# A sandwich-norm layer of linear attention and a gated FFN: loads of two units moved ahead, and the order of the engines' work around the last blocks of a slot

## The chip, the cores and the metric

The kernel runs on one core of one Trainium2 chip. The metric is the device time of one execution in microseconds (us). The engines are TensorE (PE), VectorE (DVE), ScalarE (ACT), GpSimd (POOL) and SyncE (SP); SP here issues nearly all DMAs.

## The reference

`x` has the shape (4, 1024, 512), float32. What is computed, cut to what matters:

```
x = x + layernorm(attention(layernorm(x)))
x = x + layernorm(ffn(layernorm(x)))

attention: qkv = x @ w_qkv.T + b_qkv; 16 heads of 32; chunks of 128 tokens
  inter = (q * decay_q) @ S
  intra = ((q @ k.T) * dmask) @ v
  S = lam**128 * S + (k * decay_k).T @ v      (from chunk to chunk)
  out = (inter + intra) @ w_out.T + b_out
ffn: wq = w rounded to float8_e4m3 and back, for gate, up and down
  out = ((silu(x @ gate * gate_scale) * (x @ up * up_scale)) @ down) * down_scale
```

## The kernel before

The 4096 tokens are 16 units of 256 tokens (two tiles of 128, the index `t` or `c`); four units make a sequence. Float32 operands of matmuls are split into two float16 halves, `hi` (written by ScalarE) and `lo` (the rest, written by GpSimd or VectorE), so a product takes two or three matmuls. The order of work is written out by hand, for each engine by itself, and each engine runs its list in that order; semaphores (`x_lo_d`, `h_d`, ...) tie the lists together.

There are four stages.

- **ahead(k)**, k = 0 to 13 (`LEAD` = 14), one unit each: `x` is normalised (`moments_x`, `inverse_std_x`, `x_normalise`, `x_hi`, `x_lo`, two units before it is needed), turned by a DMA transpose (`turn_x`), projected to q, k (four banks, `project_qk(k, 0..3)`, line 692) and v (`project_v`, line 707), split, and written to DRAM (`spill_q`, `spill_k`, `spill_kd`, `spill_v`). Beside it the twelve pieces of the FFN's weights are loaded (`load_piece`) and rounded (`magic`, `rounded_sum`, `rounded`), their squares taken on ScalarE (`square(n)`, line 438, in unit n + 2) and summed by PE with a matrix of ones (`sum_squares`, line 671, between q/k and v of unit n + 2); the maxima of the sums (`norms`) set a scale of the FFN's values.
- **early(s)**, s = 0, 1: attention of unit s, projection of unit s + 14, and in early(1) the output projection (`project`, line 776) and first residual of unit 0.
- **slot(s)**, s = 2 to 15: attention of unit s, output projection of u = s - 1, and the FFN of v = s - 2. In slots 16 and 17 there is no attention, in 17 no projection either.
- In a slot PE runs `scores(0, 0)`, `carry_and_state(0)`, six blocks `gate_up(v, 0..5)` (line 799; a gate half and an up half of 16 matmuls each) with the remaining attention and `project` between them, and `down(v, 0)`, `down(v, 1)` (line 813).

The state of the attention goes from chunk to chunk: `carry_and_state(s, c)` on PE gives q times state and the new part of the state, VectorE adds it (`carry_and_state`, lines 1249 and 1258), ScalarE and VectorE split it (`state_hi` line 509, `state_lo` line 1269). A fourth of the chunks have no carry or no state to make: the first chunk of a sequence has no carry, the last makes no state, which is in slots 3, 7, 11 and 15.

The parts that the change and the prediction touch:

- `load_unit(s)` on SP (lines 327 to 351) brings unit s back from DRAM in twelve DMAs: eight of `stacks` (line 340), two of `qn` (344), one of `vva` (348) and a transpose of `kt` (350). It waits for the buffers (of unit s - 2), for s = 0 and 1 instead for the weights' staging to be over, and for the spills of unit s. SP runs its list in order, so what stands behind it is issued when its twelve DMAs are. Units 0 and 1 have buffers of their own. `load_x(n)` brings `x` of unit n.
- In `gate_up(v, i)` PE waits for `silu(v, i - 1)` (ScalarE, line 543) before the gate half and for `product(v, i - 1)` (VectorE, line 1329) before the up half. `h_hi(v, i)` (ScalarE, 549) and `h_lo(v, i)` (GpSimd, 963) split the product.
- `down(v, 0)` waits at its start for the last product and for `h_lo(v, 4)`, and within it for `h_hi(v, 5)` and `h_lo(v, 5)`:

```
if t == 0:
    pe.wait_ge(h_d, 6 * v + 6)
    pe.wait_ge(h_lo_d, 6 * v + 5)
```

- `residual(u, t)` (GpSimd, 955) makes x1; `x1_moments` (VectorE), `inverse_std_of(LN_X1, ...)` (GpSimd, 887 to 894), `x1_hi` (ScalarE, 441) and `x1_lo` (GpSimd, 959) normalise and split it, `turn_x1` (SP) turns it for `gate_up`. `out_sum`, `o_max`, `scale_o`, `o_hi`, `o_lo` (VectorE 1279 to 1307, ScalarE 520) do the same for the attention's output, `turn_o` (SP, 293) turns it for `project`.

## Time and profile before

| | us |
|---|---|
| runs: median of 3 (lowest to highest) | 1053.86 (1053.73 to 1054.44) |
| the profiled execution, its own time | 1055.15 |
| its span | 1053.4 |
| PE busy | 962.4 (91%) |
| VectorE busy | 684.1 (65%) |
| GpSimd busy | 687.5 (65%) |
| ScalarE busy | 527.3 (50%) |
| `ahead`, up to the first scores of unit 0 | 0 to 274 |
| `early` | 274 to 348 |
| slots 2 to 15 | 348 to 974 |
| slots 16 and 17, and the end | 974 to 1053 |

The span is the time from the first to the last instruction of the profiled execution; the time of that execution is 1.75 us more. A timeline row has the start in us, the duration in us of the whole group (`x24` is a group of 24 instructions in a row), engine, line, operation, output<-inputs, and in brackets how long the engine stood idle before it and what released it. For SP a duration is the time in which the instruction is being issued, not that of the transfer. Matmuls overlap: the next one begins some 0.15 us before the modelled end of the last, so start to start is the measure of PE's work, and the idle time in brackets is that much shorter than what the wait costs.

### The profile page before, as it was taken

What the parts mean: (1) busy time and instruction counts of PE and PEld (TensorE: products, weight loads), DVE (VectorE), ACT (ScalarE), POOL (GpSimd) and SP (SyncE); (2) the same over time, 40 slices, a digit from 0 to 9 for tenths busy, and PEclk for the clock granted to TensorE, in tenths of its full rate; (3) what the DMA queues carried; (4) which work ended last, traced back from release to release, by engine and by line L of the source; (5) the groups of instructions that cost most, each with busy time, mean ns of one, the idle gap of its engine ahead of it and who ended that gap; (6) DMA issues with size and microseconds to landing.
All of it is one profiled execution on the core that took longest, in us unless ns stands there. A gap on an engine that the chain in (4) does not pass through costs nothing.

```text
span 1053.4 us, 21805 instructions
## 1 busy us (share of the span) xinstructions
PE 962.4 (91%) x8388; PEld 704.9 (67%) x8388; DVE 684.1 (65%) x1340; ACT 527.3 (50%) x997; POOL 687.5 (65%) x839
## 2 busy tenths in 40 slices
PE   1987989999777899999999999999999999999996
PEld 1755757777555577676776767767677686766764
DVE  6757766775475776576767657677766776756322
ACT  3534746675444554563545645456454464544421
POOL 2649887887555566685666857658576685856633
PEclk9988999999889899999999999999999999999999
DMA  9567889989999869387492864929559395621100
GB/s 341 134 206 202 247 210 227 245 209 216 244 226 229 162 136 191 76 156 128 107 189 76 165 118 114 184 75 170 112 123 166 87 169 112 130 61 41 38 24 21
DMA packets 297496, 159.79 MB, mean 152 GB/s; under 512 B 141616, under 2 KB 272688, under 8 KB 297264
## 3 DMA queue, kind: packets, MB, share of 16 engines
q1 hardware_dynamic: 296672, 157.86, 67.6%
q8 instruction: 66, 1.08, 0.5%
q10 hardware_dynamic: 720, 0.54, 0.2%
q14 instruction: 38, 0.31, 0.1%
HBM read 82.86 MB, written 41.94 MB: 118 GB/s over the span
## 4 chain that ended last, share of the span: by engine, by line
PE 58%; ACT 12%; DVE 9%; issue 8%; POOL 6%; SPq 5%; DMA 2%; POOLq 0%; DVEq 0%; ACTq 0%
PE bank L799 20%; PE bank L813 16%; PE att L776 8%; PE bank L707 4%; PE bank L692 4%; ACT w_pool L543 3%; PE att L692 3%; ACT y L441 2%; DVE w_pool L1329 2%; ACT hl L441 2%; ACT att_pool L497 2%; DVE stats L1198 2%; SPq L340 1%; DMA dram_qk<-qk_hl 1%; DVE state_hl L1269 1%
## 5 line engine op out<-in xcount | busy, mean ns | idle before, releaser
L799 PE MATMUL bank<-f_pool,gate_q 128*128 128x256 f16 x1536 | 184.2, 273 | 17.7 <-ACT w_pool L543 16.7
L799 PE MATMUL bank<-f_pool,up_q 128*128 128x256 f16 x1536 | 184.5, 274 | 0.0
L813 PE MATMUL bank<-down_q,w_pool 128*128 128x512 f16 x768 | 168.5, 379 | 11.0 <-DVE w_pool L1329 10.6
L799 PEld LDWEIGHTS bank<-f_pool,gate_q 128*128 128x128 f16 x1536 | 146.9, 98 | 41.8 <-ACT w_pool L543 21.0
L949 POOL TENSOR_TENSOR att_pool<-p,att_pool 128x512 f16<-128x512 f32 x128 | 145.7, 1161 | 39.1 <-ACT att_pool L497 39.1
L799 PEld LDWEIGHTS bank<-f_pool,up_q 128*128 128x128 f16 x1536 | 150.9, 98 | 18.0
L1329 DVE SCALAR_TENSOR_TENSOR w_pool<-bank,us_t,w_pool 128x256 f32<-128x256 f32 x192 | 84.1, 479 | 120.5 <-PE bank L799 70.6
L963 POOL TENSOR_TENSOR w_pool<-w_pool 128x512 f16<-128x512 f32 x96 | 111.8, 1164 | 65.8 <-ACT w_pool L549 65.8
L887 POOL TENSOR_TENSOR rstd<-mv,eps_t 128x1 f32<-128x1 f32 (+1 forms) x112 | 27.8, 248 | 176.8 <-DVE mv L1201 158.7
L813 PEld LDWEIGHTS bank<-down_q,w_pool 128*128 128x128 f16 x768 | 73.8, 98 | 99.9 <-DVE w_pool L1329 13.0
L497 ACT CAST att_pool<-p 128x512 f16<-128x512 f32 x128 | 75.6, 618 | 91.7 <-DVE p L1239 91.7
L549 ACT CAST w_pool<-w_pool 128x512 f16<-128x512 f32 x96 | 59.0, 614 | 75.4 <-DVE w_pool L1329 75.1
L543 ACT ACTIVATE w_pool<-bank,gs_t 128x256 f32<-128x256 f32 x192 | 80.2, 468 | 31.0 <-PE bank L799 31.0
L1239 DVE TENSOR_TENSOR p<-bank,mask 128x512 f32<-128x512 f32 x128 | 82.0, 682 | 7.1 <-PE bank L720 6.7
L776 PE MATMUL att<-wout_hl,o_t 128*128 128x512 f16 x384 | 85.5, 379 | 0.0
L890 POOL TENSOR_TENSOR rstd<-rstd,eps_t 128x1 f32<-128x1 f32 (+1 forms) x112 | 71.3, 637 | 8.8
L692 PE MATMUL bank<-o_t,w_pool 128*128 128x256 f16 x432 | 53.8, 289 | 22.5 <-DVE w_pool L1129 22.5
L1218 DVE SCALAR_TENSOR_TENSOR kd<-att,bqk,decay_k 128x256 f32<-128x256 f32 x56 | 24.4, 476 | 71.0 <-POOL kd_hl L924 57.2
L1338 DVE TENSOR_TENSOR w_pool<-bank,ds_t 128x512 f32<-128x512 f32 x32 | 22.1, 692 | 73.8 <-PE bank L813 73.8
L441 ACT ACTIVATE w_pool<-w_pool,rstd 128x512 f32<-128x512 f32 x32 | 26.0, 813 | 84.6 <-POOL rstd L894 84.6
L776 PEld LDWEIGHTS att<-wout_hl,o_t 128*128 128x128 f16 x384 | 37.6, 98 | 41.9
L692 PEld LDWEIGHTS bank<-o_t,w_pool 128*128 128x128 f16 x432 | 44.6, 104 | 31.1 <-issue 22.5
(139 smaller groups left out, 1823.1 us busy)
## 6 DMA issues: line engine op xcount, KB each, us to landing
xr<-in_x SPq DMA_DIRECT2D x32, 512.0 KB, 4.4
dram_qk<-qk_hl SPq DMA_DIRECT2D x64, 256.0 KB, 5.3
att_pool<-dram_qk SPq DMA_DIRECT2D x64, 256.0 KB, 6.8
f_pool<-dram_qk SPq DMA_DIRECT2D x64, 256.0 KB, 7.0
dram_v<-vv SPq DMA_DIRECT2D x32, 256.0 KB, 2.7
dram_kd<-kd_hl SPq DMA_DIRECT2D x32, 256.0 KB, 3.1
qn_pool<-dram_qk SPq DMA_DIRECT2D x32, 256.0 KB, 7.7
out_x<-w_pool SPq DMA_DIRECT2D x32, 256.0 KB, 2.1
```

The costliest lines, as they stand in the source:

```text
L441: return nc.scalar.activation(dst, src, ACT.Identity, scale=rstd[:, ln, 0, t:t + 1], bias=rstd[:, ln, 1, t:t + 1])
L497: nc.scalar.copy(pr_hl[:, 0, heads(g)], by_head(p32[:, g % 2])).then_inc(p_hi_d, 1)
L543: ins = nc.scalar.activation(sil[:, j], b_gate[:, j * TOK:(j + 1) * TOK], ACT.Silu, scale=gs_t[:, 2 * i + j:2 * i + j + 1])
L692: ins = nc.tensor.matmul(qk_bank(n, i)[:, j * TOK:(j + 1) * TOK], (wqkv_hi, wqkv_lo)[a][:, k, o * P:(o + 1) * P], x_mov(n)[:, b, k], start ...
L776: ins = nc.tensor.matmul(b_y[t], o_t[:, a, k, t * P:(t + 1) * P], wout_hl[:, b, k], start=(k == 0 and n == 0), stop=(k == KT - 1 and n == 2))
L799: ins = nc.tensor.matmul(b[:, j * TOK:(j + 1) * TOK], w[:, k, o * P:(o + 1) * P], x1_hl[:, v % 2, part, k], start=(k == 0 and part == 0), ...
L813: ins = nc.tensor.matmul((b_gate, b_up)[t][:, :], h_hl[:, part, k, t * P:(t + 1) * P], down_q[:, k], start=(k == 0 and part == 0), stop=(k ...
L890: nc.gpsimd.tensor_tensor(rstd[:, ln, 0, cols], rstd[:, ln, 2, cols], eps_t[:, 1, cols], ALU.pow).then_inc(pow_d[ln], 1)
L949: nc.gpsimd.tensor_tensor(pr_hl[:, 1, heads(g)], by_head(p32[:, g % 2]), pr_hl[:, 0, heads(g)], ALU.subtract).then_inc(p_lo_d, 1)
L963: nc.gpsimd.tensor_tensor(h_hl[:, 1, 2 * i:2 * i + 2].rearrange("p k t -> p (k t)"), h32[:, i % 2], h_hl[:, 0, 2 * i:2 * i + 2].rearrange( ...
L1239: nc.vector.tensor_tensor(by_head(p32[:, g % 2]), by_head(b_s[g % 2][:, :]), mask[:, heads(g)], ALU.mult).then_inc(p_d, 1)
L1329: ins = nc.vector.scalar_tensor_tensor(out=h32[:, i % 2, j * TOK:(j + 1) * TOK], in0=b_up[:, j * TOK:(j + 1) * TOK], scalar=us_t[:, 2 * i ...
```

## The change

No instruction is added or removed; what changes is where in each engine's list the steps stand, and one wait.

- SP: `load_unit(0)` stands behind unit 8 of `ahead` and no longer behind unit 12; `load_unit(1)` stands behind unit 13, ahead of the spills of v and kd of unit 13, and no longer behind them.
- PE: `sum_squares(0)` to `(5)` stand one unit later; `(6)` stays in unit 8, the rest stay. `norms(0)` on VectorE stands in unit 7 and no longer in unit 6.
- early: on ScalarE `y_normalise` stands behind `k_hi(n, 2)`, and `x1_hi` behind the last `probs_hi` and `state_hi`. On GpSimd `residual` stands behind `probs_lo(s, 1, 0)`, and `inverse_std_of(LN_X1)` and `x1_lo` behind `probs_lo(s, 1, 1)`. On VectorE `x1_moments` stands behind `carry_and_state(s, 1)` and around the last `v_sum`, `state_lo(s, 1)` before `o_max(s, 0)`.
- slot: on PE `carry_and_state(s, 1)` stands behind `gate_up(v, 4)`, and `down` waits for `silu(v, 5)` in place of `product(v, 5)`. On ScalarE `silu(v, 3)` stands before `probs_hi(s, 1, 0)`, `silu(v, 4)` before `x1_hi(u, 1)`, `state_hi(s, 1)` behind `silu(v, 5)`. On VectorE `carry_and_state(s, 1)` stands behind `product(v, 4)`, `state_lo(s, 1)` behind `scale_o(s)`.

```diff
--- before.py
+++ after.py
@@ -204,6 +204,12 @@
         def squares(n):
             buf = o32 if n % 2 else y32
             return buf[:, :].rearrange("p t d -> p (t d)").bitcast(F16)[:, 0:I]
+
+
+
+        SUMMED = {3: (0,), 4: (1,), 5: (2,), 6: (3,), 7: (4,), 8: (5, 6), 9: (7,), 10: (8,), 11: (9,), 12: (10,),
+                  13: (11,)}
+        NORMS = {7: 0, 10: 1}
 
 
         def x_src(n):
@@ -397,8 +403,10 @@
             turn_x(1)
             for k in range(LEAD):
                 ahead(k)
-                if k == LEAD - 2:
+                if k == LEAD - 6:
                     load_unit(0)
+                if k == LEAD - 1:
+                    load_unit(1)
 
             for s in range(units + 2):
                 n, u, v = s + LEAD, s - 1, s - 2
@@ -408,7 +416,7 @@
                     spill_kd(n - 1)
                 if v >= 1:
                     store(v - 1, 0)
-                if s + 1 < units:
+                if 2 <= s + 1 < units:
                     load_unit(s + 1)
                 if v >= 1:
                     store(v - 1, 1)
@@ -595,17 +603,17 @@
                 q_hi(n, 0)
                 probs_hi(s, 0, 1)
                 q_hi(n, 1)
+                k_hi(n, 2)
                 if u >= 0:
                     y_normalise(u, 0)
                     y_normalise(u, 1)
-                k_hi(n, 2)
                 probs_hi(s, 1, 0)
+                k_hi(n, 3)
+                probs_hi(s, 1, 1)
+                state_hi(s, 1)
                 if u >= 0:
                     x1_hi(u, 0)
                     x1_hi(u, 1)
-                k_hi(n, 3)
-                probs_hi(s, 1, 1)
-                state_hi(s, 1)
                 o_hi(s)
 
             def slot(s):
@@ -632,21 +640,21 @@
                 if projects:
                     y_normalise(u, 1)
                 h_hi(v, 2)
+                silu(v, 3)
                 if attends:
                     probs_hi(s, 1, 0)
-                silu(v, 3)
                 if projects:
                     x1_hi(u, 0)
                 h_hi(v, 3)
                 if attends:
                     probs_hi(s, 1, 1)
+                silu(v, 4)
                 if projects:
                     x1_hi(u, 1)
-                silu(v, 4)
-                if attends:
-                    state_hi(s, 1)
                 h_hi(v, 4)
                 silu(v, 5)
+                if attends:
+                    state_hi(s, 1)
                 h_hi(v, 5)
                 if attends:
                     o_hi(s)
@@ -803,7 +811,7 @@
 
             def down(v, t):
                 if t == 0:
-                    pe.wait_ge(h_d, 6 * v + 6)
+                    pe.wait_ge(silu_d, 6 * v + 6)
                     pe.wait_ge(h_lo_d, 6 * v + 5)
                 for k in range(IT):
                     if t == 0 and k == IT - 2:
@@ -820,8 +828,8 @@
                 project_qk(k, 1)
                 project_qk(k, 2)
                 project_qk(k, 3)
-                if 2 <= k < 14:
-                    sum_squares(k - 2)
+                for n in SUMMED.get(k, ()):
+                    sum_squares(n)
                 project_v(k, 0)
                 project_v(k, 1)
 
@@ -865,8 +873,9 @@
                 gate_up(v, 3)
                 if attends:
                     scores(s, 1, 1)
+                gate_up(v, 4)
+                if attends:
                     carry_and_state(s, 1)
-                gate_up(v, 4)
                 gate_up(v, 5)
                 if attends:
                     attend(s, 1)
@@ -1016,18 +1025,17 @@
                 if u >= 0:
                     for t in range(T):
                         inverse_std_of(LN_Y, u, t)
-                    for t in range(T):
-                        residual(u, t)
+                state_decay(s, 1)
                 probs_lo(s, 1, 0)
                 if u >= 0:
                     for t in range(T):
-                        inverse_std_of(LN_X1, u, t)
-                state_decay(s, 1)
-                if u >= 0:
-                    x1_lo(u, 0)
+                        residual(u, t)
                 probs_lo(s, 1, 1)
                 if u >= 0:
-                    x1_lo(u, 1)
+                    for t in range(T):
+                        inverse_std_of(LN_X1, u, t)
+                    for t in range(T):
+                        x1_lo(u, t)
 
             def slot(s):
                 n, u, v = s + LEAD, s - 1, s - 2
@@ -1357,10 +1365,8 @@
                     scale_wout()
                 if k == 5:
                     split_wout()
-                if k == 6:
-                    norms(0)
-                if k == 10:
-                    norms(1)
+                if k in NORMS:
+                    norms(NORMS[k])
                 k_lo(k, 2)
                 if k < 12:
                     rounded(k)
@@ -1389,16 +1395,17 @@
                 k_lo(n, 2)
                 out_sum(s, 0)
                 masked(s, 1, 0)
-                if u >= 0:
-                    for t in range(T):
-                        x1_moments(u, t)
                 k_lo(n, 3)
                 masked(s, 1, 1)
                 v_sum(n, 0)
                 carry_and_state(s, 1)
+                if u >= 0:
+                    x1_moments(u, 0)
+                v_sum(n, 1)
+                if u >= 0:
+                    x1_moments(u, 1)
+                state_lo(s, 1)
                 o_max(s, 0)
-                v_sum(n, 1)
-                state_lo(s, 1)
                 out_sum(s, 1)
                 o_max(s, 1)
                 scale_o(s)
@@ -1433,16 +1440,16 @@
                 product(v, 3)
                 if attends:
                     masked(s, 1, 1)
-                    carry_and_state(s, 1)
                     o_max(s, 0)
                 product(v, 4)
                 if attends:
-                    state_lo(s, 1)
+                    carry_and_state(s, 1)
                 product(v, 5)
                 if attends:
                     out_sum(s, 1)
                     o_max(s, 1)
                     scale_o(s)
+                    state_lo(s, 1)
                     o_lo(s)
                 y2_scale(v, 0)
                 y2_moments(v, 0)
```

Three places of the lists, as they stood and as they stand.

SP from the transpose of `x` of unit 13 on (`turn_x`, 284), which stands in unit 11 of `ahead`, before the change; `L340` to `L350` are `load_unit(0)`:

```order
L284 DMA_TRANSPOSE xr<-hl 128x8x128 x2
L274 DMA xr<-in_x 128x2x512
L325 DMA dram_v<-vv 128x1024 x2
L319 DMA dram_kd<-kd_hl 128x4x256 x2
L307 DMA dram_qk<-qk_hl 128x4x256 x2
L313 DMA dram_qk<-qk_hl 128x4x256 x2
L284 DMA_TRANSPOSE o_t<-p 128x8x128 x2
L340 DMA att_pool<-dram_qk 32x16x256 x8
L344 DMA qn_pool<-dram_qk 128x4x256 x2
L348 DMA vva<-dram_v 128x2x1024
L350 DMA_TRANSPOSE kt<-dram_kd 128x2x1024
L325 DMA dram_v<-vv 128x1024 x2
```

and after the change, in unit 8 of `ahead`, where lines are six higher (`L290` is `turn_x`, `L280` `load_x`, `L331` and `L325` the spills of v and kd, `L374` a piece of the weights, `L346` to `L356` `load_unit(0)`):

```order
L313 DMA dram_qk<-qk_hl 128x4x256 x2
L319 DMA dram_qk<-qk_hl 128x4x256 x2
L290 DMA_TRANSPOSE o_t<-p 128x8x128 x2
L346 DMA att_pool<-dram_qk 32x16x256 x8
L350 DMA qn_pool<-dram_qk 128x4x256 x2
L354 DMA vva<-dram_v 128x2x1024
L356 DMA_TRANSPOSE kt<-dram_kd 128x2x1024
L280 DMA xr<-in_x 128x2x512
L331 DMA dram_v<-vv 128x1024 x2
L325 DMA dram_kd<-kd_hl 128x4x256 x2
L374 DMA f_pool<-in_down_w 128x3x512
L313 DMA dram_qk<-qk_hl 128x4x256 x2
```

The four kinds of DMA of `load_unit(0)` now stand ahead of `load_x(12)`, the spills of v and kd of unit 8 and a piece of weights.

VectorE in a slot from `product(v, 3)` on, before (`L1329` product, `L1239` masked, `L1249` and `L1258` carry_and_state, `L1289` o_max, `L1269` state_lo, `L1279` out_sum):

```order
L1329 SCALAR_TENSOR_TENSOR w_pool<-bank,us_t,w_pool 128x256 x2
L1239 TENSOR_TENSOR p<-bank,mask 128x512 x2
L1249 TENSOR_TENSOR o<-bank,decay_q 128x512
L1258 TENSOR_TENSOR state<-bank,state_d 32x128 x4
L1289 TENSOR_REDUCE o_scale<-o 128x1
L1329 SCALAR_TENSOR_TENSOR w_pool<-bank,us_t,w_pool 128x256 x2
L1269 SCALAR_TENSOR_TENSOR state_hl<-state,state_hl 32x4x32 x4
L1329 SCALAR_TENSOR_TENSOR w_pool<-bank,us_t,w_pool 128x256 x2
L1279 TENSOR_TENSOR o<-att,o 128x512
```

and after (lines eight higher):

```order
L1337 SCALAR_TENSOR_TENSOR w_pool<-bank,us_t,w_pool 128x256 x2
L1247 TENSOR_TENSOR p<-bank,mask 128x512 x2
L1297 TENSOR_REDUCE o_scale<-o 128x1
L1337 SCALAR_TENSOR_TENSOR w_pool<-bank,us_t,w_pool 128x256 x2
L1257 TENSOR_TENSOR o<-bank,decay_q 128x512
L1266 TENSOR_TENSOR state<-bank,state_d 32x128 x4
L1337 SCALAR_TENSOR_TENSOR w_pool<-bank,us_t,w_pool 128x256 x2
L1287 TENSOR_TENSOR o<-att,o 128x512
```

`carry_and_state` stands between `product(v, 4)` and `product(v, 5)`, and `state_lo` is no longer ahead of `product(v, 5)`.

ScalarE in a slot from `h_hi(v, 2)` on, before (`L549` h_hi, `L497` probs_hi, `L543` silu, `L441` x1_hi, `L509` state_hi):

```order
L549 CAST w_pool<-w_pool 128x512
L497 CAST att_pool<-p 128x512 x2
L543 ACTIVATE w_pool<-bank,gs_t 128x256 x2
L441 ACTIVATE y<-xr,rstd 128x512
L441 ACTIVATE hl<-xr,rstd 128x512
L549 CAST w_pool<-w_pool 128x512
L497 CAST att_pool<-p 128x512 x2
L441 ACTIVATE y<-xr,rstd 128x512
L441 ACTIVATE hl<-xr,rstd 128x512
L543 ACTIVATE w_pool<-bank,gs_t 128x256 x2
L509 ACTIVATE state_hl<-state 32x4x32 x4
```

and after (lines eight higher):

```order
L557 CAST w_pool<-w_pool 128x512
L551 ACTIVATE w_pool<-bank,gs_t 128x256 x2
L505 CAST att_pool<-p 128x512 x2
L449 ACTIVATE y<-xr,rstd 128x512
L449 ACTIVATE hl<-xr,rstd 128x512
L557 CAST w_pool<-w_pool 128x512
L505 CAST att_pool<-p 128x512 x2
L551 ACTIVATE w_pool<-bank,gs_t 128x256 x2
L449 ACTIVATE y<-xr,rstd 128x512
L449 ACTIVATE hl<-xr,rstd 128x512
L557 CAST w_pool<-w_pool 128x512
```

`silu(v, 3)` stands ahead of `probs_hi`, `silu(v, 4)` ahead of the second `x1_hi`, and `state_hi` is no longer between `silu(v, 4)` and `h_hi(v, 4)`.

## Rows read from the trace of the kernel before

**Rows 1.** The page's busy time of each engine over the span

```profile
PE 962.4 (91%) x8388; PEld 704.9 (67%) x8388; DVE 684.1 (65%) x1340; ACT 527.3 (50%) x997; POOL 687.5 (65%) x839
```

**Rows 2.** Waits of PE, whole run: line, releaser, total us, times, longest

```profile
PE bank L799 <- ACT w_pool L543: 16.7, 16, 2.8
PE bank L813 <- DVE w_pool L1329: 10.6, 12, 1.0
PE bank L671 <- ACT y L438: 6.3, 2, 3.2
...
PE bank L746 <- DMA kt<-dram_kd: 4.0, 1, 4.0
```

**Rows 3.** SP timeline, projection stage: start, us in the queue, engine, line, operation

```profile
192.62 4.78 SPq L284 DMA_TRANSPOSE o_t<-p  x2
197.44 0.58 SPq L274 DMA_DIRECT2D xr<-in_x  x1
...
260.16 6.53 SPq L340 DMA_DIRECT2D att_pool<-dram_qk  x8
...
270.81 6.18 SPq L350 DMA_TRANSPOSE kt<-dram_kd  x1
...
311.74 4.49 SPq L293 DMA_TRANSPOSE o_t<-hl  x2
```

**Rows 4.** Issues of DMAs by tile: count, size, median us to landing

```profile
xr<-in_x SPq DMA_DIRECT2D x32, 512.0 KB, 4.4
```

**Rows 5.** VectorE timeline, same columns, last the idle time and its releaser

```profile
202.58 0.88 DVE L1218 SCALAR_TENSOR_TENSOR kd<-att,bqk,decay_k 128x256 f32<-128x256 f32 x2 [4.93 <-POOL kd_hl L924]
...
209.02 0.68 DVE L1198 BATCH_NORM_STATS2 stats<-xr 128x6 f32<-128x512 f32 x1
...
219.28 0.88 DVE L1218 SCALAR_TENSOR_TENSOR kd<-att,bqk,decay_k 128x256 f32<-128x256 f32 x2 [2.31 <-POOL kd_hl L924]
...
272.58 0.69 DVE L1233 TENSOR_TENSOR v<-bank,bv 128x512 f32<-128x512 f32 x1 [1.90 <-PE bank L707]
```

**Rows 6.** VectorE timeline, `o_lo` of unit 0

```profile
308.63 1.42 DVE L1307 SCALAR_TENSOR_TENSOR hl<-o,o_scale,hl 128x512 f16<-128x512 f32 x2 [0.79 <-ACT hl L520]
```

**Rows 7.** PE timeline, first attention units

```profile
280.19 4.88 PE L692 MATMUL bank<-o_t,w_pool 128*128 128x256 f16 x24
...
319.49 5.34 PE L776 MATMUL att<-wout_hl,o_t 128*128 128x512 f16 x24
...
342.67 4.35 PE L707 MATMUL bank<-w_pool,xr 128*128 128x512 f16 x12 [4.64 <-DVE qk_hl L1225]
...
358.42 2.53 PE L799 MATMUL bank<-f_pool,gate_q 128*128 128x256 f16 x16 [2.81 <-ACT w_pool L543]
```

**Rows 8.** PE timeline, ends of slots 3, 9, 16 and 17

```profile
432.46 3.84 PE L813 MATMUL bank<-down_q,w_pool 128*128 128x512 f16 x17
...
692.57 1.92 PE L799 MATMUL bank<-f_pool,gate_q 128*128 128x256 f16 x16 [0.69 <-ACT w_pool L543]
...
697.97 2.33 PE L813 MATMUL bank<-down_q,w_pool 128*128 128x512 f16 x10 [0.87 <-DVE w_pool L1329]
...
1002.71 10.53 PE L813 MATMUL bank<-down_q,w_pool 128*128 128x512 f16 x48 [0.97 <-DVE w_pool L1329]
...
1035.18 10.53 PE L813 MATMUL bank<-down_q,w_pool 128*128 128x512 f16 x48 [0.97 <-DVE w_pool L1329]
```

**Rows 9.** VectorE timeline, ends of slots 8 and 9

```profile
658.76 0.69 DVE L1338 TENSOR_TENSOR w_pool<-bank,ds_t 128x512 f32<-128x512 f32 x1 [0.46 <-PE bank L813]
...
693.70 3.31 DVE L1269 SCALAR_TENSOR_TENSOR state_hl<-state,state_hl 32x128 f16<-32x128 f32 x4 [0.21 <-ACT state_hl L509]
697.04 0.88 DVE L1329 SCALAR_TENSOR_TENSOR w_pool<-bank,us_t,w_pool 128x256 f32<-128x256 f32 x2
```

**Rows 10.** POOL timeline, `h_lo(v, 4)` of slots 3 and 9

```profile
430.42 1.16 POOL L963 TENSOR_TENSOR w_pool<-w_pool 128x512 f16<-128x512 f32 x1
...
695.36 1.20 POOL L963 TENSOR_TENSOR w_pool<-w_pool 128x512 f16<-128x512 f32 x1
```

4 lines of the change are left out of this document (2 added, 2 removed).

## The prediction

> **What bounds the kernel now.** I read the page first, then PE's waits, then timelines. PE is busy for 91% of the span [rows 1], so the question is where the other 9% lies and whether PE is what the rest waits for. PE's waits [rows 2] name three places: line 799 waits 16 times for ScalarE's SiLU and line 813 12 times for VectorE's product, which is once or twice a slot; line 671 waits for a square; line 746 waits for a load. One slot shows how the first two lie [rows 8]: the sixth gate block starts at 692.57 after an idle time, `down` at 697.97 after another. The group before goes on by 0.15 us of modelled end, so start to start they cost 0.84 us (the gate block was due at 689.98 + 1.75 = 691.73) and 1.02 us (block and attention would have let `down` start at 696.95).
>
> The projection stage is another matter. There VectorE and GpSimd form a loop: GpSimd's lower half of kd of a unit lets VectorE do k of the next, whose v sums and moments of `x` let GpSimd go on. VectorE's k of unit 10 starts at 219.28, that of unit 9 at 202.58, both after waiting for GpSimd, so a unit takes 16.70 us there [rows 5]. PE's own work of a unit is 16.3 us. So PE is not what sets the pace of units 3 to 11, though from unit 12 on it comes last: the last v sum waits 1.90 us for PE and ends at 273.27 [rows 5].
>
> **The ninth unit's load.** Before, SP issued `load_unit(0)` from 260.16 to 276.99 [rows 3], and PE's first attention waited for it: the longest wait of its kind is 4.0 us [rows 2], and projection of unit 14 began at 280.19 [rows 7]. Now these 16.8 us of issuing stand behind the transpose of unit 8's turn, which ends at 197.4 [rows 3]. What stands behind is late by as much. The one that hurts is `load_x(12)`: issued at 197.44 and 4.4 us to landing [rows 3, 4], it is read by VectorE at 209.02 [rows 5], so it has 7.2 us to spare. 16.8 - 7.2 = 9.6: the loop is held up by 9.6 us, once. (The spills of unit 8 are late too, but ScalarE's copies that wait for them have 4 us before GpSimd wants them, behind the late moments; so they don't add.) I bound this by 5 us (an issue that takes 12 us) and 17 us (nothing to spare). Against it stand 0.8 us that the loop got back where unit 6's squares had held PE and with it the v sum.
>
> Of the squares' own waits (6.3 us for one tile [rows 2], and as much for the other) the path gets nothing but that: they lie on PE while VectorE and GpSimd have their own pace. Where it helps is at the end of the stage, where PE is last. PE would reach the last v sum 6 us earlier than before if nothing were late; with the loop 9 us late, and PE starting unit 11 cold after a wait of some 11 us for its turned `x`, I put the last v sum at 279.3, 6.0 us later than 273.27. Its bounds are 3.8 (loop alone) and 9.6 (all of the delay).
>
> **Up to slot 2.** From there the load no longer counts: norms, scores and state take 1.2 us, and projection of unit 14 starts at 280.5, where it was 280.19. ScalarE's v copy of unit 13, which waited until 279.5 for a spill behind the load, isn't later either; I take early(0) to end 1.2 us earlier, at 302.3. Then the second load: before, PE waited for it in early(1), and projection of unit 0 started at 319.49 [rows 7]. Now it is issued right behind `turn_x(15)` at about 282, and its last transpose lands 20.6 us later, just as PE comes. So the chain is attention's end, sums and scale to `o_lo` (before 303.5 to 310.05 [rows 6]), two transposes: before they were issued at 311.74 in 4.49 us, because SP was still at its spills [rows 3]; now at once, about 2.6 us, and 1 us to land. 302.3 + 6.5 + 3.6 = 312.4, so 7.1 us are gained there.
>
> From that projection to the second gate block of slot 2 it was 358.42 - 319.49 = 38.9 us [rows 7]. The wait of 4.64 us for k of unit 15, and one of 1.7 for scores, go, since k and the probabilities no longer stand behind x1 on ScalarE; but x1 itself comes later: `residual` now behind the probabilities (0 + 15.3 to 17.8 from the projection), moments at 20, splits at 23 to 26, turned at 29.3, and ScalarE's SiLU behind `o_hi` and the copies of unit 15 at 36.0. That is 2.9 us less. In sum **10.0 us** by slot 2. Bounds: 3 (the load costs 17) and 20 (it costs nothing).
>
> **The slots.** Now SiLU of block 3 stands before the probabilities, of block 4 before the second x1, and PE has carry and state between blocks 4 and 5: the sixth gate block finds its SiLU (done at about 690.6 where PE comes at 691.7), so 0.84 us go. `down` could then start at 696.95 - 0.84 = 696.1. It still waits for `h_lo(v, 4)`, whose chain on GpSimd runs without a gap from the residual on and isn't changed; it ends at 695.36 + 1.20 = 696.56 [rows 10]. So `down` starts at 696.6 and not 697.97 [rows 8]: **1.36 us** for each of the ten slots with a state to make. VectorE's last product was late because `state_lo` before it took 3.31 us [rows 9]; it is out of the way now, the product follows PE. In slots 3, 7, 11 and 15 `down` started at 432.46 [rows 8], while `h_lo(v, 4)` ended at 430.42 + 1.16 = 431.58 [rows 10]: 0.8 us each. 13.6 + 3.2 = 16.8. Bounds: 10 (only the gate block's wait in ten slots, and little more) and 26 (GpSimd not binding).
>
> `state_lo` takes 3.31 us beside GpSimd's work, and that work 1.20 us where it otherwise takes 1.16 [rows 9, 10]. The Trainium skill (SBUF — State Buffer, "Who interferes with whom") says that a VectorE instruction with two SBUF inputs contends with a GpSimd one that reads SBUF, under an exclusive lock. By that rule moving `state_lo` gives GpSimd back 0.04 us on each of two instructions, and `down` would start some 0.1 us earlier still, 1 us in ten slots, for 1022.6 in place of 1023.6; the sum above leaves that out.
>
> Slot 16: `down` starts at 1002.71 [rows 8]; with SiLU 4 ahead of x1 the chain through x1's split and `h_lo(v, 4)` ends at about 1000.35, 2.4 us earlier. Slot 17: `down` starts at 1035.18 behind the product [rows 8]; now SiLU is enough, 1.1 us. Together 3.5. The tail behind the last `down` is unchanged.
>
> **The sum** is 10.0 + 16.8 + 3.5 = 30.3 us. The profiled execution took 1055.15 and would take 1024.9; the median of the runs is 1.3 us below it, which gives **1023.6 us**.
>
> **The rivals.**
> - The ninth unit's load is absorbed (its DMAs are issued faster, or the late `x` isn't waited for). For it: before, the same load behind unit 12 delayed nothing that PE wanted but itself. Against: SP's list has 11 us of issuing in each 16.7, and the margin of `x` is 7.2. Then the stage ends 4.9 us earlier than before and early gains 20: 1013.6. Chance 0.14.
> - The delay passes whole, or is nearer 17 us, since DMA is already busy there: early gains 0 to 4, 1031. Chance 0.14.
> - The slots give little: another wait takes the place (GpSimd's chain starts later because the reordered ScalarE feeds it later). For it: GpSimd has no gap there. Then 0.5 us a slot: 1036. Chance 0.08.
> - Slower: the end of the slot on VectorE becomes the bound. `state_lo` now stands before `o_lo` and `y2_scale`; `y2_scale` must be over before PE's next gate block. Before, it ended at 659.45 [rows 9], 6 us ahead of PE's block. It decides from 6 us of lateness on; 8 us would cost 2 us in each of 14 slots instead of 1.2 gained: 1053.9 - 13.5 + 28 = 1068. Even at 3.31 us `state_lo` can't use up 6. Chance 0.03.
> - The change does nothing measurable (the waits only move): 1053.9. Chance 0.01.
>
> That leaves 0.60 for the forecast, 1017 to 1030 of itself. **Range** 1012 to 1036: the first three rivals are inside or at its ends. A measurement of this kernel can tell about 0.2%, 2 us, from no change: faster 0.96, same 0.01, slower 0.03.
>
> **What would show it.** Right: in the profile after, VectorE's first moments behind unit 9 wait for `xr<-in_x` by about 10 us, and k of unit 10 starts near 228; the waits of PE for `kt` are gone; the projection of unit 0 starts near 312; slots take 43.2 us and not 44.6, line 799 no longer waits for SiLU in the sixth block, and `down` waits shortly for `h_lo`. Wrong: no wait of VectorE there (first rival), an end of the stage beyond 283 (second), slots over 44 us (third), gate block 0 waiting for `y2_scale` (fourth).

## The result, and the profile after

The changed kernel takes **1037.09 us** (median of 4 runs, 1036.04 to 1038.4), the kernel before 1053.8 (4 runs, 1052.91 to 1054.44). The ratio is 0.984, with a 95% interval of 0.983 to 0.986. So it is faster by 16.7 us, where 30.3 were forecast, and 1037.09 lies above the upper end of the range, 1036. The profiled execution took 1037.88 us, its span is 1036.1.

A few moments divide the gain. Where `down` of a slot starts is a good marker, because PE's order is fixed. (All times are from the start of the span.)

| moment | before | after | forecast |
|---|---|---|---|
| VectorE's k of unit 10 | 219.28 | 231.42 | 228 |
| last v sum of unit 13 | 272.58 | 288.13 | 278.6 |
| PE: projection of unit 14 | 280.19 | 290.09 | 280.5 |
| PE: output projection of unit 0 | 319.49 | 324.95 | 312.4 |
| PE: second gate block of slot 2 | 358.42 | 361.94 | 348.4 |
| `down` of slot 2 | 388.62 | 389.44 | |
| `down` of slot 15 | 963.40 | 949.46 | |
| `down` of slots 16, 17 | 1002.71, 1035.18 | 986.56, 1017.88 | |
| end of the span | 1053.4 | 1036.1 | |

(The forecast named 279.3 against 273.27, the end of that v sum before; 6.0 us later in either count.) From `down` of slot 2 to the end it was 664.8 us and is 646.7: 18.1 us gained, 14.8 of them up to `down` of slot 15, where most slots take 43.2 us, and 3.4 in slots 16 and 17. Up to there nothing is gained: 0.8 us are lost. By the marker that the prediction used, the second gate block, the early part is 3.5 us later instead of 10.0 earlier. **That is 13.5 us of error, and the whole of the miss**; 9.6 of them are there at the projection of unit 14 (9.9 us later, where 0.3 was forecast).

PE's waits over the whole run, after (line, releaser, total us, times, longest), against [rows 2]:

```profile
PE bank L679 <- ACT y L446: 18.6, 2, 14.8
PE bank L821 <- POOL w_pool L972: 8.4, 15, 1.0
PE att L700 <- DVE qk_hl L1233: 8.4, 3, 7.1
PE bank L807 <- DMA f_pool<-hl: 4.4, 1, 4.4
...
PE bank L746 <- DVE state_hl L1277: 2.2, 2, 1.5
```

The waits for the product, second in [rows 2], are gone; of the 16 for SiLU one is left, of 1.0 us, in slot 2; and `down` waits 15 times for GpSimd instead, as forecast. The waits for the loads of kd are gone too. (The 7.1 us at line 700 lie at 84 us and go with the moved sums of squares: with these back, in `split_no_squares`, that wait is 2.0 us at the longest.) But one wait for a square is now 14.8 us long. It has to be followed backwards. First SP's list, after, from unit 8's turn on (start, us, line, operation), against [rows 3]:

```profile
191.56 4.17 SPq L290 DMA_TRANSPOSE o_t<-p  x2
195.91 6.22 SPq L346 DMA_DIRECT2D att_pool<-dram_qk  x8
...
206.78 6.98 SPq L356 DMA_TRANSPOSE kt<-dram_kd  x1
213.81 0.58 SPq L280 DMA_DIRECT2D xr<-in_x  x1
214.43 0.94 SPq L331 DMA_DIRECT2D dram_v<-vv  x2
...
218.47 1.54 SPq L313 DMA_DIRECT2D dram_qk<-qk_hl  x2
```

The load holds SP from 195.91 to 213.76, 17.85 us. Behind it stand, in this order, x of unit 12, the spill of v of unit 8, and at 218.47 the spill of q of unit 9. Each has a reader. ScalarE, after, in unit 10 (last the idle time and its releaser):

```profile
219.10 1.27 ACT L497 CAST vv<-v 128x512 f16<-128x512 f32 x2 [16.37 <-DMA dram_v<-vv]
220.27 0.83 ACT L469 ACTIVATE q<-bank,bqk 128x256 f32<-128x256 f32 x2
226.17 0.62 ACT L474 CAST qk_hl<-q 128x512 f16<-128x512 f32 x1 [5.07 <-DMA dram_qk<-qk_hl]
...
229.18 1.48 ACT L446 ACTIVATE y<-down_q 128x1536 f16<-128x1536 f16 x1
230.56 0.82 ACT L482 ACTIVATE qk_hl<-att,bqk 128x256 f16<-128x256 f32 x2
```

The upper half of v of unit 9 overwrites `vv`, so it waits for the spill of unit 8, until 219.10. The next copy but one, q of unit 10, waits for the spill of q of unit 9, until 226.17. Behind it in ScalarE's list stand square 8 and the upper half of k. The same stretch of ScalarE in the kernel before, which the prediction did not read:

```profile
208.53 1.22 ACT L489 CAST vv<-v 128x512 f16<-128x512 f32 x2 [4.08 <-DVE v L1233]
...
213.08 0.62 ACT L466 CAST qk_hl<-q 128x512 f16<-128x512 f32 x1 [2.41 <-DMA dram_qk<-qk_hl]
...
216.09 1.48 ACT L438 ACTIVATE y<-down_q 128x1536 f16<-128x1536 f16 x1
217.47 0.82 ACT L474 ACTIVATE qk_hl<-att,bqk 128x256 f16<-128x256 f32 x2
```

The second row there is the one that decides: **the copy of q already waited 2.41 us for its spill before the change.** That spill had nothing to spare. After, the copy is 13.09 us later (226.17 - 213.08), k's upper half too (230.56 - 217.47). VectorE and PE, after:

```profile
218.40 0.69 DVE L1206 BATCH_NORM_STATS2 stats<-xr 128x6 f32<-128x512 f32 x1 [10.59 <-DMA xr<-in_x]
...
231.42 0.88 DVE L1226 SCALAR_TENSOR_TENSOR kd<-att,bqk,decay_k 128x256 f32<-128x256 f32 x2 [5.06 <-ACT qk_hl L482]
...
239.21 0.69 DVE L1241 TENSOR_TENSOR v<-bank,bv 128x512 f32<-128x512 f32 x1 [1.90 <-PE bank L715]
```
```profile
230.71 1.46 PE L679 MATMUL bank<-y,ones 128*128 128x512 f16 x3 [14.76 <-ACT y L446]
```

VectorE's wait for x, forecast at about 10 us, is there with 10.59; in [rows 5] there was none. But x lets VectorE go on at 218.40, and k then waits another 5.06 us, for ScalarE's upper half of k. The path of x, which the prediction followed, goes through GpSimd:

```profile
220.18 0.83 POOL L896 TENSOR_TENSOR rstd<-mv,eps_t 128x2 f32<-128x2 f32 x1 [13.00 <-DVE mv L1209]
...
226.87 1.15 POOL L925 TENSOR_TENSOR qk_hl<-q,qk_hl 128x512 f16<-128x512 f32 x1 [0.52 <-ACT qk_hl L474]
227.98 2.26 POOL L933 TENSOR_TENSOR kd_hl<-kd,kd_hl 128x512 f16<-128x512 f32 x2
```

GpSimd waits 13.00 us for the moments of x, and behind them the late copy of q costs it only 0.52 us. Before, k of unit 10 started 1.26 us after GpSimd's split of kd (219.28 and 218.02). So by this path alone k could have started at 227.98 - 0.52 + 1.26 = 228.7: an estimate from these rows, since no run has the x late and the spills in time. Two delays of nearly the same length lie side by side, and the spills' is the one that ends last. And PE, which has finished q and k of unit 10, stands 14.76 us in front of the sum of square 8, with v of unit 10 behind it. From there on PE, which needs 16.3 us of work for a unit, is last, and the stage ends at 288.13. The stretch in which it restarts (PEclk is the granted clock, in shares of 2.4 GHz; at 0.5 it is at 1.2):

```profile
core 0: us, PE busy (x) PEld busy (x) DVE busy (x) ACT busy (x) POOL busy (x), PEclk, DMA share, GB/s
215.00:232.00 17.00, 2.24 (x13) 1.07 (x12) 8.33 (x12) 7.71 (x15) 10.47 (x10) 0.61 1.05 276
232.00:248.00 16.00, 16.00 (x108) 10.85 (x107) 10.81 (x17) 9.73 (x19) 9.00 (x9) 0.88 0.73 198
248.00:264.00 16.00, 16.00 (x123) 11.76 (x121) 8.05 (x15) 10.25 (x20) 14.02 (x15) 1.00 0.72 170
```

After a wait in which it did 2.24 us of work PE is granted 0.88 on the mean and does 108 matmuls in 16 us, where it does 123 at 1.00. That is some 2 us more on the path.

The end of slot 9, after, against the row of 697.97 in [rows 8]:

```profile
690.74 10.52 PE L821 MATMUL bank<-down_q,w_pool 128*128 128x512 f16 x48 [0.39 <-POOL w_pool L972]
```

It waits 0.39 us, for GpSimd's `h_lo(v, 4)` and not for VectorE, and the slot took 43.25 us (690.74 less 647.49 in slot 8), where it was 44.6.

### The profile page after: what moved, and what is told of

The parts are those of the page before. It is cut to its first block, busy times and chain, and to the rows that moved or that the text cites. A ratio compares the mean times of both kernels' runs of the same rounds, so it can differ in the third digit from the quotient of the medians.

```text
span 1036.1 us, 21805 instructions
## 1 busy us (share of the span) xinstructions
PE 955.5 (92%) x8388; PEld 704.4 (68%) x8388; DVE 664.6 (64%) x1340; ACT 526.3 (51%) x997; POOL 686.2 (66%) x839
## 4 chain that ended last, share of the span: by engine, by line
PE 48%; POOL 27%; DVE 8%; issue 8%; ACT 3%; SPq 2%; DMA 2%; POOLq 0%; DVEq 0%; ACTq 0%
PE bank L821 16%; PE bank L807 13%; PE att L784 8%; POOL att_pool L958 5%; POOL w_pool L972 4%; POOL hl L968 3%; POOL rstd L899 3%; PE bank L700 3%; PE bank L715 2%; POOL xr L964 2%; POOL rstd L903 2%; DVE stats L1206 2%; POOL vv L942 2%; DMA dram_qk<-qk_hl 2%; PE att L700 2%
## 5 line engine op out<-in xcount | busy, mean ns | idle before, releaser
L700 PE MATMUL bank<-o_t,w_pool 128*128 128x256 f16 x432 | 51.7, 282 | 22.0 <-DVE w_pool L1137 21.8
```

The lines of the kernel that those rows point to most:

```text
L700: ins = nc.tensor.matmul(qk_bank(n, i)[:, j * TOK:(j + 1) * TOK], (wqkv_hi, wqkv_lo)[a][:, k, o * P:(o + 1) * P], x_mov(n)[:, b, k], start ...
```

## The experiments

Theory A: the load behind unit 8 makes three transfers late, not one: x (10 us), and the spills that ScalarE's copies of v and q wait for (13 us); ScalarE's list carries that to PE, which stands in front of a square. Rival B: the x alone. Rival C: not the load, but the moved squares or the new order of early(). Each kernel below is given by its edit against the changed kernel, or against `load0_split`, a kernel of the first experiments that became the base of the later ones. "k10" is the start of VectorE's k of unit 10, "v13" of the last v sum, "project 0" of the output projection of unit 0.

**Where the load stands: `load0_back`, `x_first`, `load0_split`.**

```diff
-                if k == LEAD - 6:
+                if k == LEAD - 2:        # load0_back
                     load_unit(0)
```
```diff
-                if k + 3 < units:
+                if k + 3 < units and k != LEAD - 5:        # x_first
                     load_x(k + 3)
...
                 if k == LEAD - 6:
+                    load_x(k + 4)
                     load_unit(0)
```
```diff
-                if k == LEAD - 6:
-                    load_unit(0)
+                if k >= LEAD - 6:        # load0_split
+                    load_unit_0(k)   # stack 3 + 3 + 2, qn 1 + 1, v, kt at k = 12
```

> The changed kernel with load_unit(0) back behind unit 12, as before; load_unit(1) stays behind unit 13 and all else as changed. Theory A (the ninth unit's load holds the whole stage back by some 15 us): VectorE's k of unit 10 is back near 219, the last v sum of the stage near 270 to 273; but the load now comes in front of the first attention again, so projection of unit 14 starts near 280 as before. Its 16.8 us and those of load_unit(1) follow each other, so projection of unit 0 starts near 312 to 315 and the total is 1024 to 1028, 9 to 13 us below the changed kernel. Rival B (the early order of ScalarE, VectorE and GpSimd or the moved squares lost the time, not the load): the stage ends near 283 to 288 as in the changed kernel, and the total stays at 1035 to 1038.

Measured 1029.22 us (0.9775 of before, 0.9761 to 0.979). k10 217.60, v13 271.56, projection of unit 14 at 278.40, project 0 at 316.80. As theory A says up to the end of the stage; project 0 came 2 us above its range, and the total 1 us above its own. Rival C is out: squares and early order are all there, and the stage ends where it did.

> The changed kernel with one DMA moved: the load of x of unit 11 and then of unit 12 are issued in the order of before, the latter (load_x of unit 12) just ahead of load_unit(0) and not behind it. Nothing else moves. Theory of the prediction (only this x has too little to spare): VectorE's wait of 10.6 us for xr goes, k of unit 10 starts at 219 to 221, the last v sum ends near 272 and the total is 1023 to 1026. Theory A (the spills of unit 8 and 9 are as late, and with them ScalarE's v and q copies and square 8): the wait for xr goes, but v_hi(9) still waits until about 219 and q_hi(10) until about 226, PE still waits over 8 us for square 8, k of unit 10 starts at 226 to 231 and the total is 1033 to 1037.

Measured 1037.24 us (0.9847, 0.9832 to 0.9862), the changed kernel's time. VectorE, ScalarE and PE of this kernel:

```profile
208.76 0.68 DVE L1207 BATCH_NORM_STATS2 stats<-xr 128x6 f32<-128x512 f32 x1
...
231.88 0.88 DVE L1227 SCALAR_TENSOR_TENSOR kd<-att,bqk,decay_k 128x256 f32<-128x256 f32 x2 [16.79 <-ACT qk_hl L483]
```
```profile
219.42 1.27 ACT L498 CAST vv<-v 128x512 f16<-128x512 f32 x2 [15.45 <-DMA dram_v<-vv]
...
226.64 0.62 ACT L475 CAST qk_hl<-q 128x512 f16<-128x512 f32 x1 [5.21 <-DMA dram_qk<-qk_hl]
```
```profile
231.17 1.46 PE L680 MATMUL bank<-y,ones 128*128 128x512 f16 x3 [12.98 <-ACT y L447]
```

The moments of x start at 208.76 without a wait: the very lateness that the prediction priced at 9.6 us is removed. k10 is at 231.88 (231.42 in the changed kernel), and the wait is now all for ScalarE. **With x in time nothing is gained**: the spills alone hold k10 as long. This is the run that decides against the prediction's reading that the spills don't add. It doesn't say that the x was harmless: alone it would have held k10 until about 228.7, by the estimate above.

> The changed kernel with the twelve DMAs of load_unit(0) spread: three of the stack behind unit 8's turn, three behind unit 9's, two and one of qn behind unit 10's, the other of qn and v behind unit 11's, the transposed load of kd behind unit 12's, where no load of x comes any more. Each group is 2.3 to 3 us of issuing where SP had some 5 us to spare in a unit. Theory A: no wait of VectorE for xr over 1 us, k of unit 10 near 219, the last v sum at 270 to 273, projection of unit 14 at 274 to 278 (it needn't wait for the load as before), projection of unit 0 at 306 to 313: total 1020 to 1026, the fastest yet. Rival (SP has no such room: turns come late by each group and PE waits for turned x in every unit): k of unit 10 at 224 or later, total 1030 to 1036.

Measured 1021.25 us (0.9702, 0.9686 to 0.9718). k10 218.15, v13 272.08, projection of unit 14 at 274.03, project 0 at 307.45. All as theory A had it. The same twelve DMAs, 16 us faster than in one piece, from SP's list:

```profile
196.55 1.54 SPq L368 DMA_DIRECT2D att_pool<-dram_qk  x3
198.13 0.49 SPq L280 DMA_DIRECT2D xr<-in_x  x1
198.67 0.94 SPq L331 DMA_DIRECT2D dram_v<-vv  x2
202.47 0.94 SPq L325 DMA_DIRECT2D dram_kd<-kd_hl  x2
...
259.24 2.52 SPq L380 DMA_TRANSPOSE kt<-dram_kd  x1
```

**The change in halves: `slots_only`.** The kernel before with ScalarE's, PE's and VectorE's lists of `slot()` and the wait of `down` as changed, nothing else.

> The kernel before with the changed order of the slots alone (ScalarE's, PE's and VectorE's lists in slot(), and the wait of down on SiLU instead of on h). The prologue, the loads, the squares and the early slots are those of before. If slots and prologue add up: projection of unit 0 at 319.5 as before, the second gate block of slot 2 at 358.4, slots of 43.2 us and the end 18 us earlier: 1035 to 1037, about the changed kernel's time, which says that all its gain is the slots'. If the slots gain only together with loads further ahead: 44 us a slot and over 1042.

Measured 1032.58 us (0.9814, 0.9797 to 0.9831): faster than the whole change by 4.5 us by the medians (the intervals of the two ratios just overlap, 0.9831 and 0.9826), and 2.4 us below my range. From `down` of slot 2 to the end 646.7 us, as in the changed kernel. So the slots' edits carry all of the gain, and the rest of the change takes some of it back: 4.5 us by the medians, of which 2 may be chance: with the same lists up to there k10 is 219.28 before and 216.90 here, and between 217.8 and 219.7 in the profiled executions of the kernels with the spread load.

**PE's own part: `sq8_behind_v`.** Against the changed kernel, in PE's list of a unit:

```diff
-                for n in SUMMED.get(k, ()):
-                    sum_squares(n)
+                if k < 10:
+                    for n in SUMMED.get(k, ()):
+                        sum_squares(n)
                 project_v(k, 0)
                 project_v(k, 1)
+                if k >= 10:
+                    for n in SUMMED.get(k, ()):
+                        sum_squares(n)
```

> The changed kernel with the sums of squares 8 to 11 behind the v projection of their unit in PE's list and not ahead of it. Loads, ScalarE's, VectorE's and GpSimd's lists are unchanged, so unit 10 is as late: ScalarE still waits for the spills, VectorE's k of unit 10 starts near 231. If PE's wait of 14.8 us for square 8, with v of unit 10 behind it, carries a part of its own: PE does v of unit 10 during the wait, isn't last from there on, the units go on at 16.7 us from 231 and then 14.4 and 14.9 us, the last v sum starts at 284 to 285 in place of 288.1, and the total falls by 3 to 4 us, to 1033 to 1034. If VectorE's lateness alone sets the end: 288 and 1037 as before.

Measured 1031.14 us (0.9795, 0.9777 to 0.9814): 6.0 us less, where I expected 3 to 4. k10 is nearly as late as in the changed kernel (230.14), but v13 is 280.25. From k10 to v13 that is 50.1 us against 56.7 in the changed kernel, and 53.3 in the kernel before. So of the 15.55 us by which v13 is late, 12.1 are there at k10, where the spills' delay is the last to end (the x alone would have made some 9.4 of them), and 3.4 come behind it (56.7 - 53.3), through PE's place in front of the square. That PE caught up 3.2 us on the kernel before I had not expected.

**What the other parts are worth: `split_no_squares`, `split_no_early`, `split_load1_back`.** Each is `load0_split` with one part of the change undone: the delays of the sums and norms, the three lists of `early()`, the place of `load_unit(1)`.

> The kernel with the spread load (load0_split, 1021.3) with the sums of squares back at a delay of two units each and VectorE's norms in unit 6. PE again waits some 6 us for each of two squares (in units 7 and 8). If these waits lie on PE alone, as the prediction had it: the last v sum still ends near 272 and the total is 1020 to 1022. If they hold v sums and so the loop: k of unit 10 comes 1 to 3 us later and the total is 1023 to 1025.

Measured 1020.42 us (0.9692, 0.9674 to 0.971): no difference from 1021.25. PE waits 5.7 and 3.4 us for squares again, and the stage ends at 272.06, as with the sums moved. This part of the prediction holds: those waits lie beside VectorE's and GpSimd's loop.

> The kernel with the spread load (load0_split, 1021.3) with the lists of early() on ScalarE, GpSimd and VectorE as before (x1 ahead of k of unit 15 and of the probabilities). The projection of unit 0 should start as there (near 307.5), and then PE should wait again for k of unit 15 (4.6 us before) and for scores (1.7), against x1 turned earlier. By the prediction's sum this order is worth 2.9 us: 1023 to 1025. If x1 behind the probabilities costs as much as it gives: 1020 to 1022.

Measured 1024.46 us, from 1022.83 to 1026.93 in four runs (0.9731, 0.9707 to 0.9756): the order of `early()` is worth about 3 us by the medians, but the intervals of the two kernels overlap (0.9718 and 0.9707). Inside the profiled executions, from project 0 to `down` of slot 2, it is 68.9 us against 65.2 in `load0_split`. PE's wait for k of unit 15 is back (3.0 us for line 739).

> The kernel with the spread load (load0_split, 1021.3) with load_unit(1) back in slot 0, behind the spills of unit 13. Unit 0's load stays spread. PE waits for the second load in early(1) again (4.0 us before, in front of the carry). By the prediction (7.1 us of its early gain come with this load and the turns behind it): projection of unit 0 near 313 in place of 307.5, total 1025 to 1028. If the spills of unit 13 are not later and attention has its own pace: 1021 to 1023.

Measured 1022.29 us (0.971, 0.9695 to 0.9725): 1.0 us, which the intervals don't tell from nothing, and below the 1025 to 1028 that the prediction's sum would make it. PE waits 3.9 us for the load of kd again and project 0 starts at 310.47, 3 us later, but `down` of slot 2 only 1.1 us later (373.76 against 372.63): from project 0 to the first gate block it is 29.1 us in place of 31.0. What takes the 2 us up there I did not follow.

**How much room the spills have: `load0_half`.** `load0_split` with `{8: (0, 1, 2), 9: (3, 4, 5), 10: (6, 7)}` replaced by `{8: range(8)}`: all of the stack behind unit 8.

> The kernel with the spread load (load0_split, 1021.3), but all eight DMAs of the stack behind unit 8's turn (some 4.5 to 6 us of issuing in place of 1.5), the rest as there. This measures how much room there is. Read now from the kernel before: ScalarE's q_hi(10) waited 2.4 us for the spill of q of unit 9, so that spill has nothing to spare but SP's own idle time of 2.9 us ahead of spill_kd(8), and k another 0.9. So 3 to 4.7 us more of issuing should make k of unit 10 late by 0 to 1 us, and little more at the end: 1021 to 1023. If spill and x have 4 and 7.2 us to spare, as the prediction had it: nothing at all, 1020.5 to 1021.5, k of unit 10 at 218. If a burst of DMAs slows the spills behind it by more than its own issuing: k at 221 or later, 1024 to 1028.

Measured 1029.64 us (0.9769, 0.9756 to 0.9783). Neither the prediction's margins nor my new ones (0 to 1 us) hold; the third reading does, and more. SP and ScalarE of this kernel:

```profile
196.38 6.27 SPq L368 DMA_DIRECT2D att_pool<-dram_qk  x8
202.69 1.75 SPq L280 DMA_DIRECT2D xr<-in_x  x1
204.49 1.17 SPq L331 DMA_DIRECT2D dram_v<-vv  x2
...
209.15 4.15 SPq L313 DMA_DIRECT2D dram_qk<-qk_hl  x2
```
```profile
213.28 1.22 ACT L521 CAST vv<-v 128x512 f16<-128x512 f32 x2 [10.02 <-DMA dram_v<-vv]
...
218.98 0.62 ACT L498 CAST qk_hl<-q 128x512 f16<-128x512 f32 x1 [3.74 <-DMA dram_qk<-qk_hl]
```

The eight DMAs take 4.7 us more than the three, but what stands behind them is slower too: x is issued in 1.75 us and not 0.49, q's spill in 4.15 and not 1.62, and v's spill, issued at 204.49, is in at 213.28. k10 starts at 224.22, 6.1 us later than in `load0_split`. Five stack DMAs more behind unit 8 cost 8.4 us in the end.

**Which edit of the slots carries them: `silu_back`, `silu_pe_back`, `state_lo_back`, `h_wait_back`, `state_lo_and_h`.** All against `load0_split` (1021.3).

```diff
                 h_hi(v, 2)                  # silu_back, ScalarE
-                silu(v, 3)
                 if attends:
                     probs_hi(s, 1, 0)
+                silu(v, 3)
...
-                silu(v, 4)
                 if projects:
                     x1_hi(u, 1)
+                silu(v, 4)
```
```diff
                     carry_and_state(s, 1)   # state_lo_back, VectorE
+                    state_lo(s, 1)
                 product(v, 5)
...
                     scale_o(s)
-                    state_lo(s, 1)
```
```diff
-                    pe.wait_ge(silu_d, 6 * v + 6)
+                    pe.wait_ge(h_d, 6 * v + 6)    # h_wait_back
```

> The kernel with the spread load (load0_split, 1021.3) with only SiLU of blocks 3 and 4 back behind the probabilities and the second x1 in ScalarE's list; state_hi stays behind SiLU of block 5, unlike in silu_pe_back. The prediction's step by itself: the sixth gate block waits 0.7 to 0.84 us for SiLU, down could start some 0.3 us later than h_lo(v, 4) lets it, so 0.3 to 0.4 us in ten slots and 0.8 or less in four: 1024 to 1028. If GpSimd's chain moves too: 1030 to 1035.

Measured 1027.12 us (0.9748, 0.9735 to 0.9761), 5.9 us more, in the range. The sixth gate block waits 0.43 us and a slot takes 43.59 us in place of 43.22: 0.37 us, as worked out from the chain to `h_lo(v, 4)`; slot 16 takes 1.07 us more.

> The kernel with the spread load (load0_split, 1021.3) with ScalarE's list of the slots and PE's carry_and_state as before; VectorE's list and the wait of down stay as changed. The sixth gate block waits again for SiLU (0.8 us). If GpSimd's chain to h_lo(v, 4) is what down waits for, most of that is hidden: 0.4 us in ten slots, 1024 to 1027. If the gate block's wait adds in full and h_lo(v, 4) comes later with it: 0.8 to 1.2 us in 14 slots, 1031 to 1038.

Measured 1041.72 us (0.9899, 0.9884 to 0.9914), 20.5 us more and above both readings. ScalarE and GpSimd at the end of a slot of this kernel:

```profile
636.85 1.26 ACT L541 ACTIVATE state_hl<-state 32x128 f16<-32x128 f32 x4 [2.69 <-DVE state L1289]
638.14 0.62 ACT L581 CAST w_pool<-w_pool 128x512 f16<-128x512 f32 x1
```
```profile
638.84 1.15 POOL L995 TENSOR_TENSOR w_pool<-w_pool 128x512 f16<-128x512 f32 x1 [1.87 <-ACT w_pool L581]
```

ScalarE's `state_hi` stands in front of `h_hi(v, 4)` again, while VectorE makes the state only behind product 4, so GpSimd waits 1.87 us for `h_hi` in front of `h_lo(v, 4)` and `down` waits 1.39 us: slots of up to 45.1 us. This kernel tests a mixture (one engine's old order with another's new one) and not the step that I meant; `silu_back` does.

> The kernel with the spread load (load0_split, 1021.3) with VectorE's state_lo(s, 1) of the slots back ahead of product(v, 5). It takes 3.3 us there beside GpSimd, so the product should end at about 2 us later than now. If down is held by h_lo(v, 4) alone since it waits for SiLU and asks for the last product only at its last two k steps: no change, 1020.5 to 1022. If the last product still sets the end of the slot, as the prediction's reason for the slots had it: 1 to 1.4 us in each of ten slots, 1031 to 1035.

Measured 1021.13 us (0.9696, 0.9684 to 0.9709), no change.

> The kernel with the spread load (load0_split, 1021.3) with down's wait on the last product (h) as before and state_lo where the change put it. The last product ends 0.3 us ahead of down there, so the wait should cost nothing in slots 2 to 15, and at most 1.1 us in slot 17, where down follows the product: 1021 to 1023. Together with state_lo_back (no change) and state_lo_and_h (30 us) this says whether the two edits cover the same wait, either alone being enough. If the wait on h costs by itself: over 1025.

Measured 1023.01 us (0.9706, 0.9692 to 0.972), 1.8 us more, in the range. The slots are the same 43.2 us; slot 17 takes 32.47 us in place of 31.32 and slot 16 37.91 in place of 37.11, which is all of it.

> As state_lo_back, and down waits again for the last product (h) in place of the last SiLU. Now down must wait for product(v, 5) behind state_lo: 1 to 1.4 us in each of ten slots, 1031 to 1035, whichever of the two views of state_lo_back is right. If it stays at 1021 to 1023, the product isn't late and neither edit of the pair did anything.

Measured 1051.72 us (0.998, 0.9967 to 0.9993; 12 runs from 1046.8 to 1054.5): 30.5 us more than `load0_split`, where each edit alone is worth 0 to 2, and far above both readings. Most of that is plain in the trace: VectorE and PE of this kernel,

```profile
638.30 1.81 DVE L1301 SCALAR_TENSOR_TENSOR state_hl<-state,state_hl 32x128 f16<-32x128 f32 x4 [2.21 <-ACT state_hl L541]
640.15 0.88 DVE L1361 SCALAR_TENSOR_TENSOR w_pool<-bank,us_t,w_pool 128x256 f32<-128x256 f32 x2
```
```profile
641.08 10.53 PE L845 MATMUL bank<-down_q,w_pool 128*128 128x512 f16 x48 [2.21 <-DVE w_pool L1361]
```

`state_lo` waits 2.21 us for ScalarE's half of the state, which now comes behind SiLU 5, and holds the last product; `down` waits 2.21 us for it, 1.8 more than for GpSimd. Slots take 45.1 us and some 44.9 or 44.4; from `down` of slot 2 to the end of the span it is 671.9 us, 25.3 more than in `load0_split`. The profiled execution took 1047.7 us and was the second fastest of the twelve. In `state_lo_back` the product is as late (631.25 against a `down` at 630.34), but `down` asks for it only at its last two k steps. This kernel too is a mixture: `state_hi` and PE's state stay where the change put them, so the wait of 2.21 us isn't the one of the kernel before, where `state_lo` waited 0.21 us and took 3.31 [rows 9].

**Faster than both: `load2_first`, `load2_no_squares`.** `load0_split` with `load_unit(2)` at the head of SP's list for `early(1)`, and the same with the sums of squares as before.

> The kernel with the spread load (load0_split, 1021.3) with load_unit(2) at the head of SP's list for early(1), ahead of the spills of v and kd of unit 14, on whose copies SP stood from 305.4 to 311. It can start some 5 us earlier, so the turn of x1 of unit 0 no longer shares the DMA with it (4.3 us of issuing against 2.6 to 2.9 elsewhere). If that congestion is what PE's first gate block waits for (4.6 us for the turned x1) and the carry of slot 2 for kt (1.9): 1.5 to 3.5 us less, 1018 to 1020, the fastest. If x1 itself is late, or the spills behind the load are then missed: 1021 or above.

Measured 1020.6 us (0.9688, 0.9675 to 0.97). `down` of slot 2 starts at 370.32 and not 372.63 in the profiled execution, but the medians are 0.65 us apart: not resolved, and above the 1018 to 1020 that I gave for a gain.

> load2_first (1020.6) with the sums of squares as before. If moving the sums is worth nothing once the ninth unit's load is out of the way: 1019 to 1020.6. If PE's waits for squares cost: 1022 or more.

Measured **1019.3 us** (0.9678, 0.9665 to 0.9691), the lowest median of all, 34 us below the kernel before and 18 below the change. From 1020.6, and from the 1021.25 of `load0_split`, its interval doesn't tell it apart; that it needs none of the edits to the squares is what it shows.

## Why the prediction was wrong

The sign was right, the size was not: 16.7 us in place of 30.3. By its own steps:

- **The ninth unit's load: the step that failed.** The prediction said that "ScalarE's copies that wait for them have 4 us before GpSimd wants them, behind the late moments; so they don't add", and put only the x, with 7.2 us to spare, on the path. The x was sized nearly right: 10.59 us of waiting (9.6 worked out), and k10 at some 228.7 by its path (228 forecast). For GpSimd the sentence nearly holds as well: the copy of q costs it 0.52 us. But behind that copy in ScalarE's list stand the upper half of k, which VectorE waits for, and square 8, which PE waits for, and neither goes through GpSimd. The copy of q already waited 2.41 us for its spill, so the lateness passed whole: 13.1 us at ScalarE, 12.1 at k10, where 8.7 were forecast. `x_first` shows that this delay stands by itself: with the x in time k10 is as late.
- **The end of the stage.** "PE would reach the last v sum 6 us earlier than before if nothing were late": PE was the one that lost most. Its sum of square 8 was moved by no unit and stands in front of v of unit 10; the prediction named only a wait for the turned x. That costs 3.4 us against before, and 6.6 against what `sq8_behind_v` makes of nearly the same lateness. This is the spills' work too: square 8 is late through ScalarE's copy of q and not through the x, and PE waits 12.98 us for it in `x_first` too. The last v sum was 15.55 us later where 6.0 were written, and 9.6 were its upper bound.
- **From there to slot 2.** The projection of unit 14 came 9.9 us later (forecast 0.3), since before 7.6 us lay between the last v sum and it, for the load, and now 2.0 do. From it to project 0: 39.3 before, 34.9 after, 31.9 forecast. From project 0 to the second gate block: 38.9, 37.0, 36.0. The second load brings 3.0 us at project 0 where the prediction gave 7.1 to it and the turns behind it, and 1.0 us (not told from nothing) in the end; the early order about 3 where it wrote 2.9. Both were measured beside the spread load.
- **The squares.** Worth nothing on the path, as written, apart from the 0.8 us that the sum took for them, which `split_no_squares` doesn't show.
- **The slots.** Four slots took 176.97 us and now take 172.27, 4.7 less, where 3 x 1.36 + 0.8 = 4.9 were forecast; `down` waits 0.38 us for `h_lo(v, 4)`, and 1.0 in every fourth. Slot 16: 39.31 to 37.10, 2.2 against 2.4; slot 17: 32.47 to 31.32, 1.15 against 1.1; the tail is unchanged at 18.2. The mechanism and the sizes are right. One reason was half right: the prediction put the product's, and so `down`'s, earlier start down to `state_lo` being out of the way. Either that move or the wait on SiLU is enough alone; with both undone slots take up to 45.1 us, though in part through another wait than before.
- **The exclusive lock.** The Trainium skill (SBUF — State Buffer, "Who interferes with whom") says that a VectorE instruction with two SBUF inputs contends with a GpSimd one that reads SBUF. By that rule the prediction would have given GpSimd 0.04 us back on each of two instructions. `state_lo` took 3.31 us before beside GpSimd's work, 1.80 in `state_lo_back`, where GpSimd works in the first 0.8 us of it, and 1.15 in `load0_split`, where GpSimd is idle: as to VectorE the trace agrees. GpSimd's two instructions (`x1_lo` and `h_lo(v, 4)` of slot 9) took 1.21 and 1.20 us before and take 1.17 each after, 0.07 us in all and of the size written; in `state_lo_back`, where `h_lo(v, 4)` still has `state_lo` beside it for 0.8 us, it takes 1.16, and nothing is seen.
- **The rivals.** The second ("the delay passes whole", 1031) was the nearest in what it describes (the third's 1036 is nearer in number, by luck: its slots over 44 us didn't come), but it too spoke of the x alone and left early 0 to 4 us of gain, where 3.5 were lost. The spills as a delay of their own and PE's place in front of the square were in no rival. (The third rival's 0.5 us a slot is 7 us in 14 slots instead of 16.8, which makes 1033.4 and not 1036.)

What stays open: how late the stage would end with the x late and the spills in time, which no run has; the 4 us by which the median of `state_lo_and_h` lies above its profiled execution; and why the catch-up behind k10 is 50.1 us where the undisturbed stage takes 53.3.

## What to carry to other kernels

Before something is put in front of a queue's list, list every transfer behind it and for each the reader that waits for it, and look in the trace whether that reader waits already: an idle time of 2.4 us with the spill as its releaser says that its margin is nothing, and 13 us of lateness went through. When two transfers are late, mending one may give nothing (`x_first`), and that doesn't make the other harmless. The margin of the one transfer that was looked at says nothing of the others, and an engine with a list in order (ScalarE here) hands the latest on to all that stand behind. A long load in a busy queue is best spread over the gaps: the same twelve DMAs held SP for 17.85 us in one place, and for 8.4 us in five, where k10 was no later than before. Where two edits remove the same wait, undo them singly and together before either is credited.

## What the runs showed of the chip

How long a DMA held SP was no fixed time in these runs; it was longer behind many others. The twelve of the load took 17.85 us in one piece, and 1.54 + 1.65 + 1.14 + 0.49 + 0.58 + 0.45 + 2.52 = 8.4 us spread; the transposed load of kd alone 6.98 us behind the others and 2.52 by itself. Behind eight of them (`load0_half`) one load of x was issued in 1.75 us in place of 0.49, two DMAs of q's spill in 4.15 in place of 1.62, and a spill of v took 8.6 us from its issue to landing (the median in that kernel is 2.7; the same spill took 6.6 in `load0_split` and 2.7 in the kernel before). The Trainium skill (DMA: Bandwidth & Descriptors, "Issuing engines are not separate DMA queues") says that the sequencer's time to start a DMA "is usually small relative to the DMA itself". For one DMA of the stack the trace agrees: behind unit 8 eight of them held SP for 6.22 us, 0.78 each, and landed 7.0 us (median) after their issue. For the transposed load of kd it doesn't: 6.98 us of issuing and 8.9 to landing, or 2.52 and 4.5 where it stood by itself. And the times add up in SP's list: the spill of q of unit 9 was issued 13.27 us later than before (218.47 against 205.20), and the copy that waits for it came 13.09 us later, so the late issue, and not a slower transfer, is what ScalarE waited for there. In `load0_half` the transfer was slower as well.
